# Second attention: the turned maxima ride in a narrow score item, and a second item of a half-step follows the value sums

## What is computed

```python
att = jnp.einsum('bhtd,bhsd->bhts', q, k) * scale
att = jnp.where(causal[None, None], att, -jnp.inf)
att = jax.nn.softmax(att, axis=-1)
y = jnp.einsum('bhts,bhsd->bhtd', att, v)
```

## Time and profile before

| | us |
|---|---|
| median of three runs | 3221.84 |
| lowest, highest run | 3221.32, 3222.61 |
| profiled execution, its own time | 3216.31 |
| its span, first to last instruction | 3214.5 |
| PE busy | 2893.3 (90%) |
| DVE busy | 2555.0 (79%) |
| ACT busy | 2044.4 (64%) |
| group 0 of the second attention begins | 822.0 |
| one later group | 92.9 |

### The profile page before, as it was taken

One profiled execution on the slowest core, in us unless ns is written; L12 is line 12 of the kernel. 1 busy time (PEld: TensorE's weight loads), 2 busy tenths in 40 slices (PEclk: granted clock), 3 DMA queues, 4 the chain that ended last, 5 costly groups with the idle time before them and its releaser, 6 DMA issues. The chain is left out here.

```text
span 3214.5 us, 66525 instructions
## 1 busy us (share of the span) xinstructions
PE 2893.3 (90%) x26519; PEld 1757.1 (55%) x26520; DVE 2555.0 (79%) x3560; ACT 2044.4 (64%) x3430; POOL 674.3 (21%) x1035
## 2 busy tenths in 40 slices
PE   5888888872899999999999999999899999999987
PEld 3555555550334443344344434434388888888975
DVE  4888888877899999999999999999265665666567
ACT  2555555540699999999999999999732232333234
POOL 1333333341222322000000000000132343332300
PEclk9999999985899999999999999999999999999999
DMA  2223333325223112222220122202121222212349
GB/s 76 69 86 89 88 91 93 93 86 102 51 55 54 36 24 54 54 54 53 54 53 17 43 54 54 53 22 87 52 68 34 71 80 73 68 42 70 103 150 309
DMA packets 252583, 230.21 MB, mean 72 GB/s; under 512 B 60908, under 2 KB 234988, under 8 KB 252012
## 3 DMA queue, kind: packets, MB, share of 16 engines
q1 hardware_dynamic: 235896, 192.32, 22.9%
q0 software_dynamic: 16384, 33.64, 3.3%
HBM read 124.21 MB, written 101.06 MB: 70 GB/s over the span
## 5 line engine op out<-in xcount | busy, mean ns | idle before, releaser
L1746 ACT ACTIVATE at_ex<-at_so,keep_exp_scale 128x512 f32<-128x512 f32 (+1 forms) x2304 | 1336.3, 679 | 203.6 <-PE at_so L1582 115.8
L1784 DVE TENSOR_REDUCE at_best<-at_p 128x2 f32<-128x1024 f32 (+3 forms) x1280 | 1284.5, 1060 | 111.1 <-PE at_p L1602 80.9
L1621 PE MATMUL at_so<-at_qs,at_ks 50*128 50x512 f16 (+3 forms) x2560 | 734.3, 352 | 33.0 <-ACT at_ex L1746 32.6
L1602 PE MATMUL at_p<-at_ks,at_qs 48*128 48x512 f16 (+3 forms) x2560 | 681.4, 358 | 50.6 <-DVE at_best L1784 49.4
L1692 PE MATMUL at_so<-at_ex,at_vs 128*32 128x256 f32 (+2 forms) x8704 | 697.2, 392 | 0.0
L2020 ACT ACTIVATE e_hh<-e_hb,e_b1now 128x512 fp32r<-128x512 f32 x256 | 176.4, 689 | 519.0 <-PE e_hb L1954 504.6
L1621 PEld LDWEIGHTS at_so<-at_qs,at_ks 50*128 50x128 f16 x2560 | 208.2, 93 | 517.6 <-ACT at_ex L1746 339.4
L1257 POOL DMA_INDIRECT e_xg<-s_xn,e_token x128 | 143.4, 1121 | 1359.5 <-DVE e_token L1252 1235.0
L1984 PE MATMUL e_ob<-e_w2h,e_hh 128*128 128x256 f32 x1024 | 295.3, 288 | 15.1 <-DVE e_og L2091 15.1
L1986 PE MATMUL e_ob<-e_w2h,e_hl 128*128 128x256 f32 x1024 | 291.8, 285 | 0.0
L1985 PE MATMUL e_ob<-e_w2l,e_hh 128*128 128x256 f32 x1024 | 291.7, 285 | 0.0
(11 more groups left out here) (267 smaller groups left out, 4498.6 us busy)
## 6 DMA issues: line engine op xcount, KB each, us to landing
s_v<-a_v SPq DMA_DIRECT2D x64, 256.0 KB, 3.0
s_qk<-a_part SPq DMA_DIRECT2D x128, 128.0 KB, 2.4
at_vs<-s_v SPq DMA_DIRECT2D x32, 512.0 KB, 10.3
s_eo<-at_empty SPq DMA_DIRECT2D x16, 1024.0 KB, 7.6
e_w<-w SPq DMA_DIRECT2D x16, 1024.0 KB, 7.7
f_rows<-s_eo SPq DMA_DIRECT2D x32, 512.0 KB, 8.0
at_qs<-s_qk SPq DMA_DIRECT2D x96, 128.0 KB, 4.4
at_ks<-s_qk SPq DMA_DIRECT2D x96, 128.0 KB, 7.2
```

The source lines that it names most:

```text
L1602: last = pe.matmul(out, qs[rows, buf, p, qt * P:(qt + 1) * P], ks[rows, buf, p, ch * SEG:ch * SEG + w], start=True, stop=ch != qc)
L1621: last = pe.matmul(so[:, v % NST, at:at + w], ks[rows, r, p, kt * P:(kt + 1) * P], qs[rows, r, p, q0:q0 + w], start=True, stop=not diag)
L1746: ev.done(act.activation(ex[:, v % NE, 0:width], so[:, v % NST, 0:width], ACT.Exp, scale=keep["exp_scale"][:, 0:1]), "ex")
L1784: last = dve.tensor_reduce(best[:, row:row + PAIRS * TT + 1:PAIRS * TT, ch], p1[:, at % NP1, :, to:to + w], AX, ALU.max)
```

## The change

Three things. The `t` item is no longer one of its own: the turned maxima go into columns 256 to 383 of the first bank of a narrow `c` item, the last narrow one of the quarter, whose bank is only half used. PE issues the transpose behind the item's second head, and it gives the item's second `s1` signal. DVE reduces the item, scales the turned maxima, and only then signals `mx`. Only where the last group has no such item left does a `t` item remain. Because the narrow item stands later in its quarter than the old place (the items at index 1, 5, 9 and 13 for quarters 0 to 3, where it was index 2), the turned maxima move in the list. Last, the second item of a half-step is issued behind the value sums.

```diff
         def stream(quarters, turned):
             out = []
             for (ahead, qc), t in zip(quarters, turned):
                 chunks = quarter(ahead, qc)
-                out += chunks[:2] + ([("t",) + t] if t else []) + chunks[2:]
+                k = [k for k, x in enumerate(chunks) if sum(w for _, _, _, w in x[4]) == HALF_BANK][-1]
+                out += chunks[:k] + [chunks[k][:5] + (t,)] + chunks[k + 1:]
             return out
...
-            work = np.cumsum([sum(w + HW for _, _, _, w in x[4]) if x[0] == "c" else 2 * P for x in items])
+            work = np.cumsum([sum(w + HW for _, _, _, w in x[4]) + (2 * P if x[5] else 0) if x[0] == "c" else 2 * P for x in items])
...
-                            masked = [("s1", out[:, w - P:w], key_mask, a, i == len(parts) - 1)]
+                            masked = [("s1", out[:, w - P:w], key_mask, a, i == len(parts) - 1 and not (turned and e == 1))]
...
-                def turn_maxima(g, it, n, items, k):
-                    _, ahead, qc = items[k]
-                    at = n + k
-                    if at >= NP1:
-                        ev.wait(pe, "mx", it, at + 1 - NP1)
+                def turn_maxima(g, n, items, k):
+                    if items[k][0] == "c" and not items[k][5]:
+                        return
+                    ahead, qc = items[k][1:] if items[k][0] == "t" else items[k][5]
                     ev.wait(pe, "neg", g + ahead, qc + 1)
-                    pe.transpose(p1[:, at % NP1, 0, 0:P], negmax[:], ident[:]).then_inc(ev.sem["s1"], 2)
+                    turned = pe.transpose(p1[:, (n + k) % NP1, 0, HALF_BANK:HALF_BANK + P], negmax[:], ident[:])
+                    turned.then_inc(ev.sem["s1"], 2 if items[k][0] == "t" else 1)
...
                         if e == 1:
-                            for k in due_now[1:]:
-                                rows_alone(g, r, use, g, LEAD, items, k)
+                            for k in paired:
+                                turn_maxima(g, LEAD, items, k)
+                            alone = due_now[1:]
+                    return alone
...
-                            half_step(g, r, use, s, p, first, items, due(2 * s + p, more))
+                            alone = half_step(g, r, use, s, p, first, items, due(2 * s + p, more))
                             behind(g, r, 2 * s + p, first)
+                            for k in alone:
+                                rows_alone(g, r, use, g, LEAD, items, k)
...
+                        if turned:
+                            turn_down(g + turned[0], turned[1], p1[0:QROWS, at % NP1, 0, HALF_BANK:HALF_BANK + P])
+                            return
                         ev.done(last, "mx")
```

More of the change, by code:

```diff
@@ L1368, in quarter @@
                     banks.append([(qt, qc, 0, (i + 1) * P)])
-                out += [("c", ahead, qc, p, parts) for parts in banks for p in range(PAIRS)]
+                out += [("c", ahead, qc, p, parts, None) for parts in banks for p in range(PAIRS)]
             return out
+        HALF_BANK = 2 * P
         def stream(quarters, turned):
@@ L1398, in attend_phase @@
         slot_of = [int(u) for u in np.maximum.accumulate([max(u, earliest.get(x[:3], 0)) for u, x in zip(slots(run), run)])]
-        kept = [k for k, x in enumerate(run) if x[0] == "o" or x[1] == 0]
-        tail, tail_slot = [run[k] for k in kept], [slot_of[k] for k in kept]
+        kept = [k for k, x in enumerate(run) if x[0] == "o" or x[1] == 0 or x[5] and x[5][0] == 0]
+        tail = [run[k] if run[k][0] == "o" or run[k][1] == 0 else ("t",) + run[k][5] for k in kept]
+        tail_slot = [slot_of[k] for k in kept]
         LEAD, RUN = len(lead), len(run)
@@ L1410, in turned_at @@
         def turned_at(items, ahead, qc):
-            return items.index(("t", ahead, qc)) + 1
+            return [k for k, x in enumerate(items) if x == ("t", ahead, qc) or x[0] == "c" and x[5] == (ahead, qc)][0] + 1
         def outputs_at(g, qc):
@@ L1587, in open_rows @@
                 def open_rows(r, use, it, n, items, k, e):
-                    _, ahead, qc, p, parts = items[k]
+                    _, ahead, qc, p, parts, turned = items[k]
                     at = n + k
@@ L1592, in open_rows @@
                         ev.wait(pe, "mx", it, at + 1 - NP1)
-                    if ahead == 1 and e == 0 and items[k] == quarter(1, 0)[0]:
+                    if ahead == 1 and e == 0 and items[k][:5] == quarter(1, 0)[0][:5]:
                         ev.wait(pe, f"in{(r + 1) % NBUF}", use, 1)
@@ L1657, in rows_alone @@
                 def rows_alone(g, r, use, it, n, items, k):
-                    if items[k][0] == "t":
-                        turn_maxima(g, it, n, items, k)
-                    elif items[k][0] == "o":
+                    if items[k][0] == "o":
                         turn_outputs(g, n, items, k)
+                    elif items[k][0] == "t":
+                        ev.wait(pe, "mx", it, n + k + 1 - NP1)
+                        turn_maxima(g, n, items, k)
                     else:
                         close(open_rows(r, use, it, n, items, k, 0) + open_rows(r, use, it, n, items, k, 1))
+                        turn_maxima(g, n, items, k)
                 def half_step(g, r, use, s, p, first, items, due_now):
@@ L1774, in normalise, with turn_down @@
                                       ALU.mult).then_inc(ev.sem["mx"], 1)
+                def turn_down(g, qc, src):
+                    ev.wait(dve, "m_in", g, G * PART * qc)
+                    ev.done(dve.tensor_scalar(mT[:, 0], src, 1.0 / LIFT, None, ALU.mult), "mstep")
+                    ev.wait(dve, "mstep", g, qc + 1)
+                    dve.scalar_tensor_tensor(out=mT[:, 1], in0=src, scalar=1.0 / LIFT, in1=mT[:, 0],
+                                             op0=ALU.mult, op1=ALU.subtract).then_inc(ev.sem["mx"], 1)
                 def stream_item(g, it, n, items, k):
@@ L1780, in stream_item @@
                     if item[0] == "c":
-                        _, ahead, qc, p, parts = item
+                        _, ahead, qc, p, parts, turned = item
                         for i, (qt, ch, to, w) in enumerate(parts):
@@ L1793, in stream_item @@
                     else:
[L1794 to L1800, removed]
+                        turn_down(g + item[1], item[2], p1[0:QROWS, at % NP1, 0, HALF_BANK:HALF_BANK + P])
                 def group(g, r, use, first, more):
```

## The result

The changed kernel takes 3388.15 us (median of four runs, 3380.69 to 3395.47) where the kernel before takes 3221.58 on the same chip: a ratio of 1.0517, interval 1.0487 to 1.0547, so 166.6 us more. The forecast was 3364, which is 142.2 more than the 3221.8 of before, in a range of 3320 to 3400. The profiled execution of after is the quickest of its four: 3380.69 us beside a span of 3378.9, 164.4 us longer than the span of before.

The account below looks back on a forecast made before the run. PE, DVE and ACT, nearly equally loaded, bound the kernel. 13 groups x (10.5 + 2.6 - 2.0) = +144.3 us, with small terms +141.9, gives 3221.8 + 141.9 = 3364 us; range 3320 to 3400.

Parts of the forecast that it names:

- mT's time and SP's shift: Maxima of (0, 2): mT complete at 1308.95, so SP's copies and everything listed behind them move 17.0 us later.
- The landing: Output of (g-1, 3) lands at 1330.5, wanted at 1320.04: DVE stalls 10.5 us in half-step 24, bounds 9.5 and 11.5.
- The alternative of 2.8 us: Half-step 24: if the output did not queue behind the load, the stall would be 2.8 us.
- The clock: After the stall, PE at the granted clock 0.5 costs 2.6 us a stall, bounds 0 and 4.4.
- The gains: Removed p1 turns, at half-steps such as 38 and 52: ACT waits less, 2.0 us a group, bounds 0 and 2.75.
- Zero besides: Second item behind the value sums, half-steps 20, 31 and 58: no gain beyond what the 2.0 us a group includes.
- The late copies: Maxima copies land after the keys of half-step 20 start: 0.7 us, bounds 0 and 1.6, vanishing in the stall.
- Rival 1: Stall in half-step 24 stays but the clock does not matter: +108 us, 3330 us; chance 0.25.
- Rivals 2 and 3: Half-step 24: 2, faster, about -20 to -30 us, chance 0.06; 3, stall 2.8 us, total within 0.2%, chance 0.02.
- Rival 4: Late load meets fill and outputs, or clock stays low longer: 15 us a group, +190, 3412 us; chance 0.07.

Follow-up runs that it names:

- the output between copies and load: Kernel after the change, with the output of (g-1, 3) moved ahead of the load, still behind the late maxima copies: ratio 0.9996.
- 22 products: Kernel after the change, with 22 products of zeros on PE at the end of half-step 24 in groups 1 to 13: 3373.20 us, ratio 1.0480.
- early maxima: Kernel after the change, with the turned maxima of (0, 2) an item of its own again in half-step 2: 3193.79 us, ratio 0.9916.
- the output first: Kernel after the change, with the output of (g-1, 3) issued ahead of the maxima copies and the load: 3228.03 us, ratio 1.0016.

## Why the prediction was right, and where its sizes were off

The mechanism, the place and the order were right; the size of the loss was 24 us short. Point by point:

- **mT's time and SP's shift.** Forecast 17.0 us; the output of (g-1, 3) goes out 32.24 us into a group on average over groups 1 to 13, forecast 1303.62 - 1288.90 + 17.0 = 31.72. In group 5 the whole list behind the first copy takes the 11.6 us of before; in groups 9 to 13 it takes up to 1.3 us more, which makes most of the half us.
- **The landing: the term that was mis-sized.** "That output lands 9.9 us after its issue" was one group's number, and the quickest of its kind. In the trace of before the 13 outputs behind a load take 9.9 to 12.5 us, 11.0 on average; in that of after, from issue to reciprocal, 8.2 to 13.4, and 10.84 on average. With the half us of the issue, the reciprocal of half-step 24 stands 43.08 us into the group, forecast 41.62, before 31.14. That is a delay of 11.9 us for the 10.5 forecast, and 1.46 x 13 = 19 us of the 24 missing. The bound of 11.5 was too narrow for the same reason: one landing with half a us either way isn't the spread of thirteen. Of the 1.46 us, 0.94 belong to the landing and 0.52 to the later issue. The other 5 us of the 24 are the balance of the smaller terms below and of the step from the profiled runs to the medians.
- **The alternative of 2.8 us**, in which SP still issues the load first but the output doesn't queue behind it, did not come, and no run built it. With the output between copies and load SP issues it at 25.1 us into the group instead of 31.8, and it costs nothing.
- **The clock.** Forecast 2.6 us a stall, taken from group 0. Measured: 1.5 in half-steps 26 to 30, and 12.73 - 11.9 = 0.8 up to the end of 25, together 2.3. That this came near 2.6 is in part luck: group 0 worked 10.3 us at the low level, while behind the stalls PE works 3.9 to 8.5 us at it. The windows of group 5 of the kernel after show how it looks (columns as above):
```profile
1382.00:1385.90 3.90, 3.87 (x23) 0.67 (x23) 3.12 (x3) 1.88 (x3) 0.00 (x0) 0.50 0.68 198
1385.90:1395.00 9.10, 8.79 (x117) 3.55 (x113) 8.55 (x12) 8.10 (x15) 0.00 (x0) 1.00 0.00 0
```
PE works again from 1382.0, at 1.2 GHz (0.50) until 1385.9, and at 2.4 GHz after. Which part of a low stretch falls on the idle time differs by group, so the price does too: group 5 has 104.0 us. Group 2 has 107.5, with a stretch at 0.5 that began 28.0 us into the group, at the end of a wait of 2.8 us for the late copies, and lasted 23.9 us. The 2.3 us are the clock's. In the profile with 22 products groups 3 to 13 have no stretch at 0.5; their reciprocal stands 11.7 us later than before and their half-steps from 31 on give 1.5 us back, which makes 103.0 us, and 103.0 us is what they take. So with the clock kept up nothing is left of the 2.3.
- **The gains.** Forecast 2.0, measured 1.66 behind the stall (0.22 more is spent ahead of it, in half-steps 10 to 18, and vanishes in it). By place as said: 38 (-0.87) and 52 (-0.81), where 0.9 each stood, and 58 and 59 give 0.78 back, where 0.6 stood. The 0.34 at 31 was there too (-0.33). Group 14, which has no stall, shows all small terms together: 0.2 in half-steps 10 to 18, 0.9 in 19 to 24 and -1.7 from 31 on make -0.6, where -1.3 was forecast.
- **"Zero besides"** for the second item behind the value sums holds for the times once the turns are folded (0.9916 with, 0.9919 without, both with early maxima); in the traces of these two it is 0.26 us, at half-step 14. It doesn't hold for the part alone, which is worth 13 us in the kernel before.
- **The late copies.** Forecast 0.7 us, to vanish in the stall. They vanish where the clock stays up, since the landing sets the stall's end. Where nothing hides them they cost 0.9 us (half-steps 19 to 24 with the output first), inside the bound of 1.6. What the term left out is PE's clock: in groups 2, 6 and 9 of the kernel after a stretch at 0.5 begins in that wait or within 3 us behind it, and with the output first such stretches make a group 5 to 6 us longer.

The table's half-steps, put together as the prediction's terms, are 13 x (11.94 + 2.3 - 1.66) = +163.6 us, for +144.3. Groups 0, 14 and 15 give -0.6 together, for -1.9. The rest up to 166.6 lies between profiled runs and medians: the spans differ by 164.4. Rival 1 fell with the filler. Rivals 2 and 3 fell with the result and its 13 waits of 11.0 us. Rival 4, 15 us a group, was nearly reached by single groups (up to 14.7) but not on average.

Three small slips of the prediction change nothing in its sum. It has PE at nine tenths from slice 10 on, while the earlier trace rows show that from slice 12. Rival 2's -20 to -30 us give 3192 to 3202, not 3195 to 3202. And the clock's upper bound of 4.4 us isn't worked out from any row.

## What to carry to other kernels

When one item of a hand-written issue list is moved, every transfer behind it moves too, so look for the buffer whose reuse is tightest behind it, and put the small output that frees it ahead of the bulk load and not behind. A landing time is taken from all its repetitions in the trace, with the mean in the sum and at least the worst as the bound; here single groups of the changed kernel went 0.9 us beyond even that (13.4 for 12.5). And the stall in this loop was paid twice, once as the stall and once, by about 2 us, at the lower clock.

## What the runs showed that was not expected

- PE's clock fell around waits of only 2.1 to 3.0 us, and then the wait became dearer than itself. Behind a wait of 0.9 us at the same place it mostly stayed up, but in groups 6 and 9 of the kernel after it fell there too, for 6.8 us each. That the times spread by this isn't shown: ten runs with the output first spread over 20 us (3217.66 to 3237.33) and four with early maxima over 4.5, but twelve of the thirteen runs of the kernel before spread over 13 on the same chip, and the one profile of that kernel has no such stretch.
- Zero products of 22 x 2 records a group gave 15 us back. The Trainium skill's page "TensorE: Matmul & The Clock Gate", section "HAM oscillation — how this bites in real kernels", says that waits recurring in a loop send each next piece back to the slow clock; the trace agrees, with at least one stretch at 0.5 in each of groups 1 to 13 (two in groups 6 and 9) and none between 832 and 2276 us before.
- SP's issue of one small output takes 0.36 us with nothing ahead and 3.3 to 7.8 us behind the load, by the 26 cases in the traces of before and after; whichever transfer comes next behind the load pays it, here the fill.
- Chip B took 3334 us for the kernel that ran in 3220 at the two other times. By the profiles of the other kernels run there, the difference lies in groups 0 to 3 (101 to 111 us each with the output between copies and load) and in what follows the last exponential of the attention (972 to 976 us, for 907 in the kernel before), not in groups 5 to 13. Its cause was not tried.
